# Value products kept in their PSUM banks, and their sum taken from there

## The reference

```python
Q = _feature_map(jnp.einsum('nsd,hdk->nshk', x, Wq[i]) + bq[i])
Kf = _feature_map(jnp.einsum('nsd,hdk->nshk', x, Wk[i]) + bk[i])
V = jnp.einsum('nsd,hdk->nshk', x, Wv[i]) + bv[i]
KV = jnp.sum(Kf * V, axis=1)
sumK = jnp.sum(Kf, axis=1)
Z = 1.0 / (Q * sumK[:, None] + 1e-06)
att = Q * KV[:, None] * Z
y = jax.nn.gelu(att.reshape(n, s, H * K) @ Wo[i] + bo[i])
x = _layer_norm(y + residual, ln1_s[i], ln1_b[i])
h = jax.nn.gelu(x @ W1[i] + b1[i])
h = jax.nn.gelu(h @ W2[i] + b2[i])
x = _layer_norm(h + residual, ln2_s[i], ln2_b[i])
```

## Time and profile before

| | us |
|---|---|
| median of three runs | 2924.09 |
| the profiled execution | 2919.42 |
| its span, first to last instruction | 2917.4 |
| TensorE busy with matmuls | 2811.2 (96%) |
| VectorE busy | 2417.1 (83%) |
| ScalarE busy | 1920.5 (66%) |
| GpSimd busy | 704.6 (24%) |
| mean granted TensorE clock, share of full | 0.985 |

### The profile page before, as it was taken

The page is one execution under the profiler, slowest core; times in us unless marked ns, Lnnn a source line. Parts: engine busy times, 40 slices in busy tenths (PEclk is TensorE's granted clock), DMA queues, the critical chain, the costliest instruction groups (busy, mean ns, idle before and its releaser), DMA issues. The chain is left out here.

```text
span 2917.4 us, 35444 instructions
## 1 busy us (share of the span) xinstructions
PE 2811.2 (96%) x12986; PEld 2324.3 (80%) x12986; DVE 2417.1 (83%) x3615; ACT 1920.5 (66%) x2839; POOL 704.6 (24%) x482
## 2 busy tenths in 40 slices
PE   5899999999999999999999999999999999999988
PEld 4688888888888888888888888888888877776777
DVE  7978898889888988888888888888989875776466
ACT  5667777776677777767776777677777763444255
POOL 2203231223122312321233123312322112100313
PEclk9899999999999999999999999999999999998999
DMA  3000101000100010101000100110010011101422
GB/s 123 20 1 28 31 5 37 22 23 19 37 22 23 19 37 12 33 19 37 12 31 21 37 6 22 35 37 6 23 32 23 2 32 41 51 1 50 179 40 36
DMA packets 62093, 92.00 MB, mean 32 GB/s; under 512 B 16480, under 2 KB 42336, under 8 KB 59744
## 3 DMA queue, kind: packets, MB, share of 16 engines
q1 hardware_dynamic: 57840, 85.46, 9.2%
q0 software_dynamic: 4080, 4.27, 0.9%
HBM read 80.24 MB, written 10.38 MB: 31 GB/s over the span
## 5 line engine op out<-in xcount | busy, mean ns | idle before, releaser
L804 PE MATMUL PS<-XTHI,WHI 128*128 128x512 f32 x1536 | 625.5, 407 | 19.5 <-DVE EX L1162 14.7
L806 PE MATMUL PS<-XTHI,WLO 128*128 128x512 f32 x1536 | 607.1, 395 | 0.0
L805 PE MATMUL PS<-XTLO,WHI 128*128 128x512 f32 x1536 | 602.7, 392 | 0.0
L1036 ACT ACTIVATE ATT<-INV,CC,CE 128x128 f32<-128x128 f32 x1024 | 432.7, 485 | 121.8 <-PE Y L846 115.5
L846 PE MATMUL Y<-WO,ATT 128*128 128x256 f32 x2048 | 455.7, 381 | 6.0 <-ACT ATT L1036 6.0
L846 PE MATMUL Y<-W2S,H 128*128 128x256 f32 x2048 | 458.1, 380 | 2.0 <-DVE T L1234 1.4
L846 PEld LDWEIGHTS Y<-WO,ATT 128*128 128x128 f32 x2048 | 391.6, 191 | 61.8 <-ACT ATT L1036 5.6
L846 PEld LDWEIGHTS Y<-W2S,H 128*128 128x128 f32 x2048 | 387.0, 190 | 55.5 <-DVE T L1234 1.8
L804 PEld LDWEIGHTS PS<-XTHI,WHI 128*128 128x128 f32 x1536 | 291.4, 190 | 84.3 <-issue 16.8
L1001 ACT ACTIVATE EX<-PS,BNEG 128x512 f32<-128x512 f32 x256 | 165.5, 684 | 292.5 <-DVE INV L1214 152.0
L806 PEld LDWEIGHTS PS<-XTHI,WLO 128*128 128x128 f32 x1536 | 290.7, 189 | 64.9
(11 more groups left out here) (211 smaller groups left out, 4786.4 us busy)
## 6 DMA issues: line engine op xcount, KB each, us to landing
STAGE<-L_attn_Wkvq SPq DMA_DIRECT2D x64, 384.0 KB, 3.1
WO<-L_attn_Wo SPq DMA_DIRECT2D x8, 1024.0 KB, 4.8
W2S<-L_attn_W SPq DMA_DIRECT2D x8, 1024.0 KB, 4.8
STAGE<-L_attn_W SPq DMA_DIRECT2D x32, 256.0 KB, 5.3
WGU<-L_ffn_r_gate SPq DMA_DIRECT2D x8, 512.0 KB, 9.8
WGU<-L_ffn_r_up SPq DMA_DIRECT2D x8, 512.0 KB, 9.5
WD<-L_ffn_r_down SPq DMA_DIRECT2D x8, 512.0 KB, 9.6
rows_in<-R SPq DMA_DIRECT2D x1, 3036.0 KB, 13.2
```

What stands on the lines that cost most here:

```text
L804: nc.tensor.matmul(out, whi[:, kc, :], xhi[:, kc, :], start=(kc == 0), stop=False)
L805: nc.tensor.matmul(out, whi[:, kc, :], xlo[:, kc, :], start=False, stop=False)
L806: ins = nc.tensor.matmul(out, wlo[:, kc, :], xhi[:, kc, :], start=False, stop=(kc == KD - 1))
L1036: ins = nc.scalar.activation(ATT[:, 2 * p + i, ss], INV[:, b, i, ss], ACT.Identity, scale=CE[:, b, k:k + 1], bias=CC[:, b, k:k + 1])
```

## The change

The product stays in the bank: the scalar_tensor_tensor writes back into `PS[:, VB + i]`, from which it reads. Two reductions of half the length take the place of one: the first from the two banks, counting the new semaphore `kv_sum`, the second over the key features in `EX`, counting `sums`. `EX[:, b, 0:2]` is no longer written or read in the stack. TensorE waits at both places for `kv_sum` of the whole pair, where it waited for `kv_mul` of one chunk.

```diff
-                free = (kf, kv_mul, wq)[which]
+                free = (kf, kv_sum, wq)[which]
...
-                        pe.wait_ge(free, 2 * n - 1 + i)
+                        pe.wait_ge(free, n if which == 1 else 2 * n - 1 + i)
...
-                        pe.wait_ge(kv_mul, last - 3 + m)
+                        pe.wait_ge(kv_sum, last // 2)
...
-                    nc.vector.scalar_tensor_tensor(EX[:, b, i, :], PS[:, VB + i, :], BA[:, 1, c:c + 1],
+                    nc.vector.scalar_tensor_tensor(PS[:, VB + i, :], PS[:, VB + i, :], BA[:, 1, c:c + 1],
                                                    EX[:, b, 2 + i, :], ALU.add, ALU.mult).then_inc(kv_mul, 1)
                 if normed1 is not None:
                     normed(*normed1)
                 if biased2 is not None:
                     z_biased(*biased2)
                 dve.wait_ge(kv_mul, 2 * n + 2)
-                nc.vector.tensor_reduce(SUMS[:, b, :], by_seq(EX[:, b, 0:4, :]), AX.X, ALU.add).then_inc(sums, 1)
+                nc.vector.tensor_reduce(SUMS[:, b, 0:2 * TS], by_seq(PS[:, VB:VB + 2, :]), AX.X, ALU.add).then_inc(kv_sum, 1)
+                nc.vector.tensor_reduce(SUMS[:, b, 2 * TS:4 * TS], by_seq(EX[:, b, 2:4, :]), AX.X, ALU.add).then_inc(sums, 1)
```

More of the change, by code:

```diff
@@ L570, in attention_stack @@
             sem(n) for n in ("w_hi", "b_neg", "clipped", "ex", "log", "inv", "y_act", "x1_hi", "h_act", "z_act", "xt_hi"))
+        kv_sum = sem("kv_sum")
         snap, kf, wq, kv_mul, sums, stat, denom, residue, recip, xt_lo, x1_lo = (
```

## The result

The changed kernel takes 3019.93 us (median of four runs, 3016.2 to 3023.19) against 2922.56 for the kernel before beside it: ratio 1.0329, 95% interval 1.0309 to 1.0348, so 97 us slower. The forecast was 84 us more and 3008 us. The profiled execution took 3023.19, with a span of 3021.2; that is 103.8 more than the span before.

The account below looks back on a forecast made before the run. TensorE was taken as the bound, with VectorE meeting it within 0.1 us at hidden chunk 2. A slot's 2.92 + 0.1 - 0.3, taken as 2.8, times 30 gave 84 us: 2924.1 + 84 = 3008 us, range 2985 to 3050.

Parts of the forecast that it names:

- The release behind bias addition and reduction: End of slots 1 to 30: hidden chunk 2 waits for kv_sum behind the bias addition, starting 2.92 us later a slot.
- The stall at pair 3: Before V of pair 3: TensorE waits 1.2 to 3.1 us, 57 us together, booked at nothing as chunk 2's stall contains it.
- The wait at chunk 2 in every fourth slot: Sign at hidden chunk 2: a new class of TensorE waits for the reduction, 1.2 to 1.9 us.
- The extra reduction: VectorE, two reductions for one: 0.06 us a pair, only pair 0's going through, so 0.06 a slot.
- The price of PSUM: VectorE's products writing into PSUM: 742 ns kept, so 0 taken, bounds -1.2 to +3.2 us a slot; costly-write rival 9%.
- What ScalarE gives back: End of the hidden layer: ScalarE catches up, begins the next slot 0.3 us earlier with VectorE, so -0.3 a slot.
- the 2.8 that I took: Sum for a slot: 2.92 + 0.1 - 0.3 = 2.7, up to 2.9 if ScalarE gives back less; 2.8 taken.
- The clock: Rival, 4%: stalls lower TensorE's clock, 2.3 us a fall; some 10 us for seven long stalls, 3077 us if every slot falls.
- one of my signs that the prediction is wrong: TensorE's granted clock was to stay at 1.00 from 150 to 2400 us; a fall inside the stack would refute the prediction.
- the range: Whole kernel's time: 2985 to 3050 us, the main case with part of the PSUM write's price; some 15 in 100 outside.

Follow-up runs that it names:

- e1: Kernel before with the reduction split in two, products still in SBUF, and both of TensorE's waits moved to the first reduction: 3017.05 us, ratio 1.0317.
- e8: The change with VectorE's pair 3 reordered: X1LO, products and PSUM reduction first, then Newton's step of pair 2, bias addition, second reduction: 2953.58 us, ratio 1.0101.
- e3: Kernel before with the reduction split, products in SBUF, and only the wait of hidden chunks 2 and 3 moved to the first reduction: 3049.03 us, ratio 1.0434.
- e6: The change with pair 3's bias addition and pair 2's first normalisation both put behind the first reduction: 3025.12 us, ratio 1.0345.
- e2: Kernel before with the reduction split in two and nothing else, TensorE waiting for the products as before: 2919.67 us, ratio 1.0000.
- e9 to e11: e8 with pair 2 also reordered, Newton's step later: 3053.41 us; kernel before with pair 2 reordered: 2976.63; kernel before with pairs 2 and 3 reordered: 2972.83.
- e5: The change with only pair 3's bias addition put behind the first reduction: 2983.80 us, ratio 1.0203.
- e4: Kernel before with the reduction split, products in SBUF, and only the wait of the value products moved to the first reduction: 2944.01 us, ratio 1.0078.
- e7: The change with TensorE making the eight transposes of the next input twice, before hidden chunk 2: 3017.65 us, ratio 1.0322.

## Why the prediction was right, and where its sizes were off

*The release behind bias addition and reduction.* Forecast 2.92 a slot, measured 2.90 from X1LO on and 2.88 from slot to slot; e1 shows that it alone is the loss, e8 that it goes when the release comes before TensorE.

*The stall at pair 3, booked at nothing.* Right as long as the clock stays up: in slot 13 VectorE is unmoved, and e3 and e6 gain nothing by removing it. It was closer than the prediction has it where the clock fell behind V of pair 3: in those four slots VectorE waited 0.9 to 2.3 us in front of X1LO. The wait at chunk 2 in every fourth slot is 2.7 us where the clock stays up, not the 1.2 to 1.9 forecast; that moves idle time, but adds none to the slot.

*The extra reduction*, 0.06 a slot, 2 us in all: e2 finds 0 within 0.13% of 2920, 4 us, and within 0.03 us by its trace.

*The price of PSUM*, 0 with bounds of -1.2 and +3.2: 8 ns a product, 0.05 a slot. The Trainium skill's 65 ns more on PSUM ("Perfetto Trace Analysis", "Optimizing Scalar/DVE Operations") would have been 0.4, an estimate; where the instruction already read from PSUM, writing there too did not add it.

*What ScalarE gives back*, -0.3: this term was wrong; it is 0. The gain arises. The last gelu of slot 13 now starts at 1166.70, with the last matmul over by 1166.28 + 0.39 = 1166.67, and VectorE begins the next slot 0.29 earlier relative to chunk 2 (L1210 and L1212 start 13.42 and 13.13 us after it in slot 8). But it doesn't reach the next chunk 2. Between pair 1 and pair 2 ScalarE's weighing waits for TensorE's output projection anyway:

```profile
882.75 3.19 ACT L1037 ACTIVATE ATT<-INV,CC,CE 128x128 f32<-128x128 f32 x8 [4.08 <-PE Y L847]
```

and behind it everything is at the old distance again, to 0.01. I had followed the chain over VectorE and left out that wait. Against the 2.8 that I took, the measured 2.89 makes 30 x 0.09, 3 us.

*The clock.* I gave it 4% as a case of its own, with 10 us for long stalls alone, and forecast that it stays at 1.00 in the stack; a fall there was one of my signs that the prediction is wrong, and there were 11. It is 14 us of the change, on top of the 30 x 2.89 = 87. It came also behind stalls of 1.8 us, for which the 2.22 us of the earlier trace rows without a fall had made me take 1.00 as granted. One wait without a fall was no bound: of some 26 waits of 1.8 us in the change's trace seven had one behind them.

87 + 14 = 101 for the profiled execution, where the spans differ by 103.8; the timed runs have 97. That the total came within the range is owed to luck in one respect: the mechanism priced the 87 at 84, but the number of falls was not foreseen. It was five in e1, with the same waits, and 27 in e3, where the falls cost 42 us; nothing in my working excluded so many.

## What to carry to other kernels

A bank that keeps an intermediate result is held until the result's last reader is done, and everything that stands in the queue between maker and reader counts. So look not at busy shares but at the distance between the release of the buffer and its next use, in each place that uses it; here it was 0.09 us with the other engine 83% busy. When a release has to come later, look for instructions that can go behind it instead of in front: one instruction put behind the reduction gave back a third of the loss, a new order two thirds. Before an instruction is put later, ask who waits for its result, engine by engine: e9 to e11 lost 54 to 135 us against the kernel before, and their traces show ScalarE waiting for a step that I had not followed.

## What the runs showed of the hardware

A scalar_tensor_tensor of 512 numbers that reads its bank took 742 ns writing to SBUF and 750 ns writing back into the same bank. A reduction of 1024 numbers took 1224 ns out of PSUM and 1208 out of SBUF.

How long TensorE stands still did not decide alone whether the granted clock fell. A wait of 2.6 us in front of chunk 2 had a fall behind it in all 22 slots of e3 in which it occurred, 1.6 us each. But none of the seven waits of 2.7 us at the same place in e1 had one, and none of three in the change. Behind the waits of 1.7 to 1.8 us there were seven falls in 26 cases in the change and five in 22 in e1. The wait of 3.0 us in front of V of pair 3, seven times in each kernel, had a fall behind it seven times in e5, six in e8, four in the change and in e4, and never in e1 and e7. What decides beside the length is open, so the number of falls has to be read from the trace of the version in question, and a forecast can only give bounds for it.
